# A vision tower's second mixture: one accumulator in DRAM in place of two, with scatters one after the other

## What is computed

```python
topk_idx, topk_w = _route(x, gate_weight, e_bias)      # 8 of 64 experts, with weights
xe = jnp.zeros((E, CAP, H)).at[sorted_e, pos].set(tok_sorted, mode='drop')
h = silu(einsum('ech,efh->ecf', xe, w1)) * einsum('ech,efh->ecf', xe, w3)
ye = einsum('ecf,ehf->ech', h, w2)
out = segment_sum(vals * flat_w[:, None], flat_t, num_segments=T)   # 592 x 256
shared = silu(x @ shared_gate.T) * (x @ shared_up.T) @ shared_down.T
return (out + shared)                                   # and the caller adds it to h
```

## Time and profile before

| what | us |
|---|---|
| median of 3 runs (lowest, highest) | 450.86 (449.02, 452.77) |
| the profiled execution, its own time | 450.0 |
| its span, first to last instruction | 446.9 |
| TensorE busy | 413.4 (92%) |
| VectorE busy | 257.8 (58%) |
| GpSimd busy | 157.0 (35%) |
| ScalarE busy | 135.9 (30%) |
| mean granted TensorE clock | 0.979 |

### The profile page before, as it was taken

One profiled execution on the slowest core, in us unless ns is written; L12 is line 12 of the kernel. 1 busy time (PEld: TensorE's weight loads), 2 busy tenths in 40 slices (PEclk: granted clock), 3 DMA queues, 4 the chain that ended last, 5 costly groups with the idle time before them and its releaser, 6 DMA issues. The chain is left out here.

```text
span 446.9 us, 8837 instructions
## 1 busy us (share of the span) xinstructions
PE 413.4 (92%) x2990; PEld 330.8 (74%) x2990; DVE 257.8 (58%) x649; ACT 135.9 (30%) x343; POOL 157.0 (35%) x129
## 2 busy tenths in 40 slices
PE   8999999889981999999999899998998999999993
PEld 5665567766761999999986489886676788888872
DVE  0548878766930012211165789997776556656545
ACT  1030068783310111121202765552401132323210
POOL 2007835540075000100362068781001156554560
PEclk9999999999995899999999999999999999999997
DMA  8763086001085367786234033430124577777462
GB/s 269 223 182 104 2 291 229 3 1 56 1 304 219 111 224 233 276 286 227 59 99 146 24 143 104 109 83 2 54 55 141 163 174 202 179 186 186 109 128 100
DMA packets 32076, 63.55 MB, mean 142 GB/s; under 512 B 6062, under 2 KB 19677, under 8 KB 29741
## 3 DMA queue, kind: packets, MB, share of 16 engines
q1 hardware_dynamic: 26381, 50.90, 36.3%
q0 software_dynamic: 5664, 12.25, 10.7%
HBM read 50.51 MB, written 12.63 MB: 141 GB/s over the span
## 5 line engine op out<-in xcount | busy, mean ns | idle before, releaser
L1850 PE MATMUL PS<-xT,w1s 128*128 128x296 f32 x224 | 60.7, 415 | 0.0
L1850 PEld LDWEIGHTS PS<-xT,w1s 128*128 128x128 f32 x224 | 41.4, 190 | 11.1 <-issue 0.2
L1723 PE MATMUL PS<-scratch,w0up 128*128 128x144 f32 (+1 forms) x256 | 38.1, 310 | 12.0 <-DVE scratch L1153 11.6
L1723 PEld LDWEIGHTS PS<-scratch,w0up 128*128 128x128 f32 x256 | 36.4, 198 | 13.9 <-DVE scratch L1153 12.5
L1799 PE MATMUL PS<-ident,scratch 128*128 128x128 f32 (+1 forms) x340 | 43.9, 281 | 1.2 <-DVE scratch L1249 1.1
L617 POOL DMA_INDIRECT scratch<-xg,idx_nxt x18 | 17.9, 996 | 72.7 <-DVE idx_nxt L1382 38.7
L1799 PEld LDWEIGHTS PS<-ident,scratch 128*128 128x128 f32 (+1 forms) x340 | 38.8, 183 | 5.6 <-DVE scratch L1249 2.4
L1243 DVE TENSOR_TENSOR_SCAN scratch<-scratch,PS 128x592 f32<-128x592 f32 x32 | 41.9, 1362 | 1.4 <-PE PS L1806 1.4
L1170 DVE COPY scratch<-PS 128x144 f32<-128x144 f32 (+1 forms) x16 | 5.1, 321 | 64.7 <-PE PS L1732 64.7
L769 ACT ACTIVATE scratch<-PS 128x288 f32<-128x288 f32 (+1 forms) x32 | 13.8, 431 | 76.5 <-PE PS L1723 76.5
L1865 PE MATMUL PS<-w1s,scratch 128*128 128x256 f32 (+1 forms) x140 | 34.8, 382 | 2.0 <-DVE h L1286 1.1
(11 more groups left out here) (326 smaller groups left out, 752.2 us busy)
## 6 DMA issues: line engine op xcount, KB each, us to landing
w0dn<-in_w0dn SPq DMA_DIRECT2D x9, 1024.0 KB, 5.8
w0up<-in_w0up SPq DMA_DIRECT2D x9, 1024.0 KB, 6.1
w0dn<-in_w SPq DMA_DIRECT2D x16, 384.0 KB, 3.6
scratch<-rows_c SPq DMA_DIRECT2D x14, 296.0 KB, 3.3
by_expert<-zeros SPq DMA_DIRECT2D x2, 1920.0 KB, 13.3
w1s<-in_w SPq DMA_DIRECT2D x14, 256.0 KB
w1s<-in_w SPq DMA_DIRECT2D x14, 128.0 KB, 3.2
w0up<-in_patchesT SPq DMA_DIRECT2D x6, 296.0 KB, 4.3
```

What stands on the lines that cost most here:

```text
L1723: last = mm(PS[:, z, (f % 2) * width:(f % 2 + 1) * width], w0up[:, s, c, f * P:(f + 1) * P], xeT[:, s, c, 0:width], start=c == 0, stop=c == 1)
L1850: last = mm(PS[:, 2 * n + j, 0:HALF], w1s[:, s, w:w + F1], xT[:, c, half(n)], start=c == 0, stop=c == 1)
```

## The change

The two DRAM accumulators become one, so that both scatters of a half add to the same rows. The first waits for both semaphores (the previous half's two scatters), the second for the first of its own half. GpSimd no longer loads the accumulator; SyncE does, behind its last expert load, once both semaphores are full. GpSimd adds token tiles 0 and 1 into `h` (128x512) and raises `acc_low`; VectorE adds tiles 2 and 3 (128x512) and 4 (80x256). SyncE's first store waits for `acc_low`. The one accumulator is zeroed in four DMAs of 192 rows.

```diff
-        acc = [nc.dram_tensor(f"acc{q}", (XROWS, D), F32, kind="Internal").ap() for q in range(2)]
+        acc = nc.dram_tensor("acc", (XROWS, D), F32, kind="Internal").ap()
...
+            for q in range(2):
+                sp.wait_ge(acc_done[q], mixed * 32 + 16 * ZEROED)
+            sp.dma_start(acc_sb[:, 0:4, :], acc[0:4 * P, :].rearrange("(t p) d -> p t d", p=P)).then_inc(acc_in, 16)
+            sp.dma_start(acc_sb[0:ROWS[4], 4, :], acc[4 * P:NT, :]).then_inc(acc_in, 16)
             for t in range(NTILE):
                 if t == 0:
-                    sp.wait_ge(acc_added, 3)
+                    sp.wait_ge(acc_low, 1)
...
                     for q in range(2):
                         pool.wait_ge(ysp_ready, hh * 2 + (2 + q + 1))
-                        pool.wait_ge(acc_done[q], hh * 16 + 16 * ZEROED)
+                        if q == 0:
+                            pool.wait_ge(acc_done[0], hh * 16 + 16 * ZEROED)
+                            pool.wait_ge(acc_done[1], hh * 16 + 16 * ZEROED)
+                        else:
+                            pool.wait_ge(acc_done[0], hh * 16 + 16 * (ZEROED + 1))
                         passed()
                         nc.gpsimd.indirect_dma_start(
-                            acc[q], bass.IndirectOffsetOnAxis(ap=idx_cur[:, s, q:q + 1], axis=0),
+                            acc, bass.IndirectOffsetOnAxis(ap=idx_cur[:, s, q:q + 1], axis=0),
                             ysp[:, q, :], None, compute_op=ALU.add).then_inc(acc_done[q], 16)
             for q in range(2):
-                pool.wait_ge(acc_done[q], mixed * 32 + 16 * ZEROED)
-                passed()
-                pool.dma_start(acc_sb[:, q, 0:4, :], acc[q][0:4 * P, :].rearrange("(t p) d -> p t d", p=P)).then_inc(acc_in, 16)
-                pool.dma_start(acc_sb[0:ROWS[4], q, 4, :], acc[q][4 * P:NT, :]).then_inc(acc_in, 16)
-            for q in range(2):
                 pool.wait_ge(xe1_in[q], mixed * 32 + 16)
+            pool.wait_ge(acc_in, 32)
+            pool.wait_ge(y1_taken, total * 6 + 13)
+            passed()
+            nc.gpsimd.tensor_tensor(h[:, 0:2, :], h[:, 0:2, :], acc_sb[:, 0:2, :], ALU.add).then_inc(acc_low, 1)
...
-            for q in range(2):
-                dve.wait_ge(acc_in, 64)
-                nc.vector.tensor_tensor(h[:, 0:4, :], h[:, 0:4, :], acc_sb[:, q, 0:4, :], ALU.add).then_inc(acc_added, 1)
-                nc.vector.tensor_tensor(h[0:ROWS[4], 4, :], h[0:ROWS[4], 4, :], acc_sb[0:ROWS[4], q, 4, :], ALU.add).then_inc(acc_added, 1)
-                dve.wait_ge(acc_added, 2 * (q + 1))
+            dve.wait_ge(acc_in, 32)
+            nc.vector.tensor_tensor(h[:, 2:4, :], h[:, 2:4, :], acc_sb[:, 2:4, :], ALU.add).then_inc(acc_added, 1)
+            nc.vector.tensor_tensor(h[0:ROWS[4], 4, :], h[0:ROWS[4], 4, :], acc_sb[0:ROWS[4], 4, :], ALU.add).then_inc(acc_added, 1)
+            dve.wait_ge(acc_added, 2)
             add_output(total * 2 + 3, it, (1, 2))
```

More of the change, by code:

```diff
@@ L80 @@
 ZEROED = 2
+ZROWS = XROWS // (2 * ZEROED)
 W1U = 2 * 2 * F1
@@ L243, in vit_tower @@
             (P, (2, HALF)), (P, (SLOTS1, NT)), (P, (NTILE, NR1 + 1)), (P, (2, 2, XGW)), (P, (2, 2 * MC)), (P, (2, D)),
-            (P, (2, MC)), (P, (2, MC)), (P, (2, NTILE, D)))
+            (P, (2, MC)), (P, (2, MC)), (P, (NTILE, D)))
         wsp = w0dn[:, :, :, :].rearrange("p s f d -> p (s f d)")[:, 0:GROUP * W1C].rearrange("p (q w) -> p q w", q=GROUP)
@@ L348, in vit_tower @@
         acc_done = [sem(f"acc_done{q}") for q in range(2)]
-        acc_in, acc_added = sem("acc_in"), sem("acc_added")
+        acc_in, acc_added, acc_low = sem("acc_in"), sem("acc_added"), sem("acc_low")
         block = ctx.enter_context(nc.Block())
@@ L587, in _ @@
                 for z in range(ZEROED):
-                    pool.dma_start(acc[q][3 * P * z:3 * P * (z + 1), :].rearrange("(p r) d -> p r d", r=3),
-                                   zeros[:, :].unsqueeze(1).broadcast_to([P, 3, D])).then_inc(acc_done[q], 16)
+                    at, n = (q * ZEROED + z) * ZROWS, ZROWS // 3
+                    pool.dma_start(acc[at:at + ZROWS, :].rearrange("(p r) d -> p r d", r=3),
+                                   zeros[0:n, :].unsqueeze(1).broadcast_to([n, 3, D])).then_inc(acc_done[q], 16)
             pool.wait_ge(inp_part, 1)
@@ L622, in _ @@
             mixed = pool.value_load(lists[0:1, LA_AT:LA_AT + 1], min_val=1, max_val=NR1 // GROUP)
+            total = pool.value_load(lists[0:1, LT_AT:LT_AT + 1], min_val=2, max_val=PAIRS_MAX - 1)
             pool.wait_ge(xg_in, ROWS_IN + 16 * (1 + NTILE + 2))
```

## The result

The changed kernel has a median of 456.48 us in 16 runs (453.86 to 458.55), the kernel before 449.0 in 16 runs on the same chip (447.47 to 452.77): a ratio of **1.0151, with an interval of 1.0126 to 1.0176**. It is slower by 1.5%. The forecast was 455.9, and 5.0 us more than before; the ratio makes it 6.8 of 449 (the medians lie 7.5 apart). The profiled execution has a span of 452.7, 5.8 more than before; its own time went from 450.0 to 454.44, since 1.7 us lie outside the span now and 3.1 did before. On the chip of the later runs, where the kernel before has a median of 437, the changed kernel was measured again: 1.010 (1.0065 to 1.0136).

A forecast was written before the change was run, and what follows sets the result against it. TensorE was taken to bound the loop at 9.66 us a half. Slip of 6.8 us, then the last landing, accumulator load, additions and stores moved the span from 446.9 to 451.9; 450.86 + 5.0 = 455.9, range 449 to 463.

The forecast's parts named there:

- TensorE hides GpSimd up to 9.66 us a half: Mixed loop: TensorE runs without a gap, so GpSimd costs nothing while its gathered rows arrive in time.
- L1: Landing time of a half's first scatter, from start of issue; taken as 5.0 us beside expert loads.
- L2: Landing time of a half's second scatter, taken as 4.5 us.
- By the landings: Mixed loop: both scatters' landings plus 0.65 us after each, forecast at 10.8 us a half.
- by GpSimd's queue: Mixed loop: first landing, second scatter's issue, two gathers and gaps, L1 + 5.66, forecast at 10.66 us a half.
- Slip 6.8 us: Mixed loop: six halves with loads, each 1.14 us longer, delay the last first scatter from 426.5 to 433.3.
- Who waits: TensorE waits at its transposes for late gathers; 0 to 2.1 us of slack, losing 4.7 to 6.8 us.
- The tail: After the loop: accumulator load ends last at 446.2, then GpSimd's and VectorE's additions and five stores, span ending at 451.9.
- The chain fits: Rival, mixed loop: scatters land in 3.9 us whatever is loaded, a half needs 9.56, not slower; 448.5 to 451, chance 0.27.
- The second scatter hit as well: Rival, mixed loop: second scatter slips into expert loads too, a half needs 12.0 us; 459 to 467, chance 0.15.
- Does not chain as it reads: Rival, scatter waits: awaited numbers are reached early, giving the time of the chain that fits; no separate chance given.
- The saving at the tail, at most 2.1: End of kernel: VectorE's accumulator additions shrink from 3.14 to 1.0 us, saving at most 2.1 us.

The follow-up runs named there:

- the last run of experiment 2: Kernel before, with one wait added: a half's first scatter also waits for the second scatter of the half before; ratio 0.9994.
- experiment 3: Changed kernel's tail with two DRAM accumulators and the scatter waits of before, only accumulator 0 loaded and added; ratio to the kernel before 0.9974.
- experiment 6: Kernel before, but SyncE loads both accumulators, GpSimd sums them early for tiles 0 to 3, VectorE adds that sum once; ratio 1.0003.
- a tiny addition: Changed kernel with all tiles added by VectorE, plus a 128x1 GpSimd addition waiting for VectorE's large one; ratio to the kernel before 1.0122.

## Why the prediction was right, step by step

**TensorE hides GpSimd up to 9.66 us a half.** Right: the wait between halves alone costs nothing, and with light loads neither do both waits.

**L1, the first landing, 5.0 in the six halves with loads.** Right in size. It was 5.5, 4.9, 5.0, 4.3, 5.5 and 4.4, mean 4.93, then 4.3 and 3.8. That loads stretch it was shown by taking them away (3.7 to 4.3 throughout). That a slipped scatter gets out of them fits the trace of the changed kernel: the scatters that started 1.2 to 2.7 us after SyncE began to issue its pair of expert loads landed after 4.9 to 5.5, the two that started 3.1 after it (halves 3 and 5) after 4.3 and 4.4. SyncE's issues of the pairs of halves 3 and 4, ahead of the first scatters at 390.78 and 400.39:

```profile
387.71 1.84 SPq L484 DMA_DIRECT2D w0dn<-in_w  x2
...
398.89 2.37 SPq L484 DMA_DIRECT2D w0dn<-in_w  x2
```

But on the later chips the means of these six are 4.9 to 5.1 in the kernels that don't slip (the last run of experiment 2, experiments 3 and 6) and 4.8 to 5.1 in those that do, so that slipping shortened them is seen on the first chip only, and that 5.0 fitted everywhere is in part luck. The estimate from the fit of the Trainium skill (DMA: Bandwidth & Descriptors, Anatomy of one DMA), 2.3 us and with the issue some 3.9, agrees with the runs with light loads (3.7 to 4.3) and falls short by 1.0 of the mean beside heavy ones.

**L2, the second landing, 4.5.** Wrong in size: 3.5 in the first two halves of the profile and 3.7 at the end. And with that the loop that closes is the other of the two that I wrote down. By the landings a half would need 4.93 + 3.6 and twice 0.8, which is 10.1; by GpSimd's queue, with my prices, it needs L1 + 5.66 = 10.6. Measured over halves 0 to 5: 62.68 / 6 = 10.45. I had taken the larger, 10.8, from the landings. The run with only the second scatter's wait shows that no first scatter has to wait for a second one's landing for the loss to arise. What the chain held up was the gathers queued behind the waiting scatter.

**Slip 6.8 us.** Measured 4.8. The sign and mechanism hold; the term was too large by 2.0. Some 0.8 of it comes from L2, which made a half 10.8 and not 10.66; 0.4 from L1; and 0.9 from the queue's own part, 5.5 on average and not 5.66, because GpSimd's gaps behind the second scatter were 0.30 to 0.43 where I had taken 0.57 (against that, 0.8 and not 0.65 passed from a landing to the waiting scatter). The short halves (9.61 and 9.68, halves 3 and 5) are those with first landings of 4.3 and 4.4. No wait for indices shows ahead of a gather, only gaps of 0.30.

**Who waits.** Right: TensorE waits at its transposes for gathers. The gather landed after 4.5 us, near the upper bound of 4.94, so the slack was 0.4, not 2.1. TensorE lost 3.9 us (437.76 to 441.70), where the forecast had 4.7 to 6.8. ScalarE waited 8.0 us in all for landings, ahead of its silu, but TensorE shows no new wait at the work that the silu feeds (L1859, L1874); so I keep the nothing that I counted for it. 1.1 us of TensorE's 3.5 at the transposes the profile gives to nobody.

**The tail.** The accumulator's load ended last, as forecast. Its terms were off both ways. The last second scatter started at 435.57, 2.3 us earlier than forecast; the load landed 5.5 us after SyncE's first issue (forecast 4.2; 4.3 in the later run where VectorE adds all); GpSimd's addition took 1.38 (forecast 1.4) and was done at 446.63, 1.5 earlier than forecast. Two terms were missing, both from GpSimd: it blocked VectorE for 0.9 us, and it moved the end of the program by 1.3. By the rows only the second is in the time: from GpSimd's end to the end of the span I had counted 3.8, and it was 6.07, so that VectorE and the stores had 1.3 to spare. These 2.3 more at the end against 1.5 less before it make the span 452.7 against the forecast 451.9. The forecast is thus closer than its terms deserve, and that is luck. So is part of the nearness of the two medians: the forecast started from 450.86, the median of three runs; from the 449.0 of the sixteen it would have been 454.0, against 456.48.

**The rivals.** The chain fits: false with the loads of this kernel, true with light ones. The second scatter hit as well: false. With heavy loads and the wait inside a half its landing was 3.5 to 4.1 wherever the profile gives it, but for one of 4.7 (half 3 of the changed kernel's second run). Does not chain as it reads: false.

**The saving at the tail, at most 2.1.** The most it gave alone was 1.1 (experiment 3), in a run whose end also came later, by 0.8 us, after the last store's issue.

## What to carry to other kernels

A wait in GpSimd's queue costs what is queued behind it: here a landing of 4.9 us stood ahead of two gathers that TensorE needed, and an engine at 34% busy became the bound. Before merging two buffers into one, add up landing, issues and gaps round the queue and compare with the period of the bounding engine, with the landing taken beside the traffic that will run then. An addition given to GpSimd at the tail has to be counted with what it blocks on VectorE and with the end of the program.

## What the runs showed of the hardware

The span ended 6.05 to 6.09 us after GpSimd's last arithmetic instruction in all five runs in which that came late: 6.07 in the changed kernel, 6.08 in its second run and in experiment 3, 6.05 with light loads, 6.09 after a tiny addition of 0.19 us. Where GpSimd ended early, 1.7 to 1.8 us passed from the last store's issue. The profile names the wait only as one for another engine's sequencer at the last line; what GpSimd does in those 6 us stays open. In experiment 6 its last addition ended 6.5 us before the end, and the end came 1.7 after the last issue.

Additions with both inputs in SBUF on VectorE and GpSimd held each other up, and the one that had started first kept its time. Where GpSimd was first, VectorE's ended 0.3 to 0.6 us after GpSimd's, whatever it would have taken (80x256 took 1.31 and 1.19 and not 0.41, 128x512 took 1.47 and not 0.69). Where VectorE was first, its 128x512 took its 0.69, and GpSimd's of the same size 1.38 us, against 1.08 in experiment 3, where GpSimd was first. The Trainium skill (SBUF — State Buffer) says that the port pair which the two share is held by one instruction at a time; the traces agree.
